# A gated state-space block and a routed expert block in one kernel: one routing pass behind the scan, D times u and the residual in PSUM, 19 weight splits inside the scan

## What is computed

```python
x = x + tanh(g_xattn) * ssm(ctx_1024, layernorm(x))
x = x + tanh(g_ffn) * moe(layernorm(x))
# ssm, per batch row: u = silu(conv(in_proj(ctx)) + conv_b); dt_lo, B, C = x_proj(u)
#   delta = softplus(dt_proj(dt_lo) + dt_proj_b)
#   state = state * exp(delta * A) + (delta * u) * B      # scan over 256 positions, 16 states
#   y = (sum over states of state * C + D * u) * silu(z)  # z = layernorm(x), transposed back at the end
# moe: logits = x @ gate_w; softmax over the best 2 of 8; sum of cw_e * (silu(x @ w0_e) * (x @ w1_e)) @ wo_e
```

## Time and profile before

| | us |
|---|---|
| median of 3 runs (340.27 to 341.49) | 341.0 |
| the profiled execution | 341.57 |
| its span, first to last instruction | 339.8 |
| set-up, to the first product of the scan | 0 to 38.3 |
| scan, to the end of the last scan instruction | 38.3 to 181.6 |
| behind the scan, to the first expert product | 181.6 to 212.5 |
| expert stage | 212.5 to 339.8 |

### The profile page before, as it was taken

How to read it: one execution, slowest core, us unless ns; L and a number is a source line. 1 busy time by engine, 2 the same in 40 slices (tenths; PEclk the granted TensorE clock), 3 DMA queues, 4 the chain that set the end, 5 groups by cost and what they waited for, 6 DMA issues and landing times.

```text
span 339.8 us, 4549 instructions
## 1 busy us (share of the span) xinstructions
PE 265.8 (78%) x1093; PEld 174.1 (51%) x1094; DVE 246.7 (73%) x450; ACT 176.8 (52%) x327; POOL 185.0 (54%) x162
## 2 busy tenths in 40 slices
PE   3976687747898857574866957999999999999960
PEld 4522142313444414232321645798899889988950
DVE  3757999999999896989995886356655655565540
ACT  2495386545476549344667061245655565566540
POOL 4001348995799759293999403234465446545331
PEclk9987558997999789696999775799999999999996
DMA  6799000000000000300007731112332333233221
GB/s 192 241 379 379 7 1 0 2 1 0 0 1 0 2 1 0 123 1 0 0 2 237 254 126 32 39 22 50 64 48 48 60 62 46 46 62 62 30 23 25
DMA packets 18910, 22.69 MB, mean 67 GB/s; under 512 B 2624, under 2 KB 14062, under 8 KB 18894
## 3 DMA queue, kind: packets, MB, share of 16 engines
q1 hardware_dynamic: 13312, 16.39, 13.9%
q0 software_dynamic: 4416, 6.03, 11.0%
q10 hardware_dynamic: 1166, 0.08, 0.2%
HBM read 17.38 MB, written 5.11 MB: 66 GB/s over the span
## 4 chain that ended last, share of the span: by engine, by line
PE 48%; DVE 20%; issue 13%; POOL 8%; ACT 5%; DMA 2%; POOLq 1%; SPq 0%; DVEq 0%; ACTq 0%
PE PD L865 10%; PE PZ L901 10%; PE PU L865 10%; PE PY L733 7%; POOL hC L390 7%; DVE states L1036 5%; DVE states L1042 4%; PE PY L887 3%; DMA xs<-in_x 2%; PE PY L695 2%; PE PZ L858 2%; PE PU L725 2%; POOL W_lo L381 1%; PE PY L847 1%; PE PU L842 1%
## 5 line engine op out<-in xcount | busy, mean ns | idle before, releaser
L390 POOL TENSOR_TENSOR hC<-states,WO 128x512 f32<-128x512 f32 x64 | 82.6, 1304 | 35.7 <-PE PY L733 20.4
L733 PE MATMUL PY<-hC,ident 128*128 128x512 f32 x128 | 78.9, 702 | 12.8 <-POOL hC L390 12.4
L1042 DVE TENSOR_TENSOR_SCAN states<-PD,states 128x512 f32<-128x512 f32 x64 | 77.5, 1212 | 0.2 <-ACT PD L541 0.2
L425 POOL DMA_INDIRECT out<-lg,y_at x23 | 36.4, 1585 | 55.8 <-ACT lg L627 52.2
L541 ACT ACTIVATE PD<-WO,Aneg 128x510 f32<-128x510 f32 x64 | 44.0, 688 | 40.0 <-DVE states L1042 35.8
L1309 DVE TENSOR_TENSOR WO_lo<-WO,WO_hi 128x512 fp32r<-128x512 f32 x46 | 29.8, 689 | 34.5 <-ACT WO_hi L620 33.9
L620 ACT ACTIVATE WO_hi<-WO 128x512 fp32r x46 | 26.5, 624 | 47.0 <-PE PZ L901 46.8
L1036 DVE TENSOR_TENSOR states<-PU,WO 128x512 f32<-128x512 f32 x64 | 43.0, 673 | 2.5 <-POOL hC L390 2.4
L725 PE MATMUL PU<-BC,sel 128*128 128x512 f32 x32 | 20.5, 640 | 28.7 <-DVE states L1036 28.7
L733 PEld LDWEIGHTS PY<-hC,ident 128*128 128x128 f32 x128 | 26.3, 224 | 29.8 <-POOL hC L390 24.5
L412 POOL DMA_INDIRECT hC<-x_rows,x_at x23 | 23.3, 1014 | 29.1 <-DVE x_at L1265 15.0
(11 more groups left out here) (221 smaller groups left out, 498.6 us busy)
## 6 DMA issues: line engine op xcount, KB each, us to landing
W<-in_L_ffn_w SPq DMA_DIRECT2D x16, 512.0 KB, 11.0
WO<-in_L_ffn_wo SPq DMA_DIRECT2D x8, 512.0 KB, 4.5
xs<-in_x SPq DMA_DIRECT2D x1, 1024.0 KB, 7.9
x_rows<-u SPq DMA_DIRECT2D x2, 512.0 KB, 2.8
out<-xs SPq DMA_DIRECT2D x2, 512.0 KB, 3.8
early<-in_ctx SPq DMA_DIRECT2D x1, 512.0 KB, 4.2
hC<-x_rows,x_at POOLq DMA_INDIRECT x23, 2.8
out<-lg,y_at POOLq DMA_INDIRECT x23, 3.8
```

The source lines that it names most:

```text
L390: pool.tensor_tensor(hC[:, n % 2, :], states[:, n % RING, :], C_rep[:, pair % C_RING, :], ALU.mult).then_inc(hc_done, 1)
L425: pool.indirect_dma_start(out=out, out_offset=bass.IndirectOffsetOnAxis(ap=y_at[:, s:s + 1], axis=0), in_=y_tile[s % 2], in_offset=None, c ...
L733: pe.matmul(PY[:, h, :], ident[:, :], hC[:, n % 2, :], start=(m == 0), stop=(m == DS - 1)).then_inc(y_done, 1)
L1042: dve.tensor_tensor_scan(states[:, n % RING, :], DEC[n % 2], states[:, n % RING, :], 0.0, ALU.mult, ALU.add).then_inc(scan_done, 1)
```

## The change

1. **Routing in one pass.** `places` and `ranks` run once, over 8 blocks of 128 rows and not twice over 4, behind the scan; `best_two` of the first half stands behind the last scan too. The two adds that make its logits (`logits_of`) stay inside, since TensorE wants the bank. `rows_hot` moves behind `places`, the slot table behind the table of rows.
2. **Skip in PSUM.** Each of the four sums in PY starts with a matmul of u by a diagonal matrix of D; the DVE instruction L1059 goes.
3. **Residual in PSUM.** TensorE puts x (`add_x`) and then the gated rows times tanh(g) (`add_gz`) into one bank; ACT copies the sum out (`x2_out`). DVE's L1070 goes, and the two halves of `turn_gz` become real matmuls.
4. **Softplus of the second half.** The relu and the 1 + e of `rounding` go from DVE to ACT, which writes the latter into PSUM.
5. **Splits.** 19 inside the scan, after steps 4, 7, ... 58 (before 24, from step 34 on after every second one), 4 on POOL behind it, 2 and 7 on DVE (before 4 and 4).
6. WARM from (2, 3, 1) to (1, 3, 1); the tables of steps are new.

```diff
+TURN_X_AT, X_OUT_AT, BASE_AT, BASE_OUT_AT = (17, 29), (22, 34), (23, 35), (28, 40)
+ADD_X_AT, ADD_GZ_AT, X2_OUT_AT = ((41, 42), (56, 57)), (43, 44), 49
+ROUTER_AT, LOGITS_AT, STATS_AT, RSTD_AT, ROOT_AT = 50, 53, (50, 51, 52), 55, 54
...
-WARM = (2, 3, 1)
+WARM = (1, 3, 1)
...
-SPLIT_AT = (4, 7, 10, 13, 16, 20, 24, 28, 32) + tuple(range(34, 64, 2))
-POOL_SPLITS = 28
+SPLIT_AT = tuple(range(4, 60, 3))
+POOL_SPLITS = len(SPLIT_AT) + 4
+DVE_SPLITS = (POOL_SPLITS, POOL_SPLITS + 2, len(SPLITS))
...
+            def x2_out(q):
+                for r in range(QB):
+                    b = q * QB + r
+                    act.wait_ge(x2_ps, b + 1)
+                    act.activation(xs[:, 2 * b:2 * b + 2, :].rearrange("p t d -> p (t d)"), PZ[r][:, :], ACT.Copy).then_inc(x2_ok, 1)
...
+            def plus_one(c):
+                act.wait_ge(relu_ok, c + 1)
+                act.wait_ge(sp_exp_ok, c + 1)
+                act.activation(DRAW[c], sp_exp[c], ACT.Identity, bias=1.0).then_inc(one_plus, 1)
...
+                if m == 0:
+                    if q:
+                        pe.wait_ge(gz_ok, h + 1)
+                    pe.wait_ge(diag_ok, 2)
+                    pe.matmul(PY[:, h, :], diag_D[:, h, :], u[:, q, h, :], start=True, stop=False)
                 pe.wait_ge(hc_done, n + 1)
-                if q and m == 0:
-                    pe.wait_ge(gz_ok, h + 1)
-                pe.matmul(PY[:, h, :], ident[:, :], hC[:, n % 2, :], start=(m == 0), stop=(m == DS - 1)).then_inc(y_done, 1)
+                pe.matmul(PY[:, h, :], ident[:, :], hC[:, n % 2, :], start=False, stop=(m == DS - 1)).then_inc(y_done, 1)
...
+            def add_x(q, r):
...
+                for l in range(2):
+                    pe.matmul(PZ[r][:, l * DX:(l + 1) * DX], ident[:, :], xs[:, q * QBLK + 2 * r + l, :], start=(l == 0), stop=False)
+
+            def add_gz(q, r):
+
+                pe.wait_ge(gz_ok, 2 * q + 2)
+                for l in range(2):
+                    for h in range(2):
+                        at = l * DX + h * P
+                        mm = pe.matmul(PZ[r][:, at:at + P], zs[:, q * QBLK + 2 * r + h, l * P:(l + 1) * P], scaled_id[:, :], start=False, stop=(l == 1 and h == 1))
+                mm.then_inc(x2_ps, 1)
...
+            for h in range(2):
+                dve.tensor_scalar(diag_D[:, h, :], ident[:, :], cols[:, 2, h:h + 1], None, ALU.mult).then_inc(diag_ok, 1)
+            dve.tensor_scalar(scaled_id[:, :], ident[:, :], tg[:, 0:1], None, ALU.mult).then_inc(gc_ok, 1)
...
-            through(RSTD_AT, BEST_AT)
-            best_two(0)
-            through(BEST_AT, PLACE_AT)
-            places(0)
-            through(PLACE_AT, NT)
-            gated(1, 0, 2)
-            gated(1, 1, 3)
+            through(RSTD_AT, NT)
+            best_two(0)
+            gated(1, 0)
+            gated(1, 1)
+            logits_of(1)
             best_two(1)
-            residual(1, 0)
-            residual(1, 1)
+            chosen_two()
+            link(dve.tensor_tensor(gap[:, :], top[:, :, 1], top[:, :, 0], ALU.subtract))
+            lower(DVE_SPLITS[0], DVE_SPLITS[1])
+            row_stats(1, 0)
+            row_stats(1, 1)
             variance(1)
+            places()
             rows_hot(dve, 0)
-            places(1)
             rows_hot(dve, 1)
```

More of the change, by code:

```diff
@@ L582, in _ @@
             act.wait_ge(c_ps, NT // 2)
-            for i in range(len(SPLIT_AT), len(SPLITS)):
+            for i in range(len(SPLIT_AT), DVE_SPLITS[1]):
                 upper(i)
+            x2_out(1)
             root(1)
@@ L588, in _ @@
             act.activation(egap[:, :], gap[:, :], ACT.Exp).then_inc(egap_ok, 1)
+            for i in range(DVE_SPLITS[1], DVE_SPLITS[2]):
+                upper(i)
             act.wait_ge(table_set, 1)
@@ L813, in _ @@
             base_logits(1)
-            through(BASE_AT[1] + 1, TURN_GZ_AT + 1)
-            turn_gz(0)
-            through(TURN_GZ_AT + 1, ROUTER_AT + 1)
-            router(0)
-            through(ROUTER_AT + 1, RANKS_AT + 1)
-            ranks(0)
-            through(RANKS_AT + 1, NT)
+            at = BASE_AT[1] + 1
+            for r in range(QB):
+                through(at, ADD_X_AT[0][r] + 1)
+                add_x(0, r)
+                at = ADD_X_AT[0][r] + 1
+            for r in range(QB):
+                through(at, ADD_GZ_AT[r] + 1)
+                add_gz(0, r)
+                at = ADD_GZ_AT[r] + 1
+            through(at, ROUTER_AT + 1)
+            router(0)
+            at = ROUTER_AT + 1
+            for r in range(QB):
+                through(at, ADD_X_AT[1][r] + 1)
+                add_x(1, r)
+                at = ADD_X_AT[1][r] + 1
+            through(at, NT)
             def keep_warm(n):
@@ L829, in _ @@
             router(1)
-            turn_gz(1)
+            for r in range(QB):
+                add_gz(1, r)
             pe.wait_ge(dbu_done, NT)
@@ L833, in _ @@
             keep_warm(WARM[0])
-            ranks(1)
+            ranks()
             keep_warm(WARM[1])
@@ L1126, in best_two, with lower @@
                 link(ins)
-                dve.tensor_tensor(mask[:, q, :, :], hot[:, q, 0, :, :], hot[:, q, 1, :, :], ALU.add).then_inc(mask_ok, 1)
+                dve.tensor_tensor(mask[:, :, :, :], hot[:, :, 0, :, :], hot[:, :, 1, :, :], ALU.add).then_inc(mask_ok, 1)
+            def lower(at, end):
+                for i in range(at, end):
+                    dve.wait_ge(W_hi_ok, i + 1)
+                    dve.tensor_tensor(lo_part(i), whole_part(i), hi_part(i), ALU.subtract).then_inc(W_lo_dve, 1)
             def mark(ins):
@@ L1181, in places @@
+                need(tiled)
+                ends = mark(dve.tensor_tensor_scan(tile_end[:, :], ones[:, 0:E], tiles[:, :], 0.0, ALU.mult, ALU.add))
                 need(chosen)
[L1182 to L1186 removed]
@@ L1210, in _ @@
-            drive(0)
-            through(0, 2)
-            relu(2)
-            through(2, 3)
-            relu(3)
-            through(3, 8)
+                summed = mark(dve.tensor_reduce(of_n(rank_f), picked[:, :, :, :, :].rearrange("p q k t e -> p (q k t) e"), AX_X, ALU.add))
+                need(ends)
+                starts = mark(dve.tensor_tensor(first_slot[:, :], tile_end[:, :], tiles[:, :], ALU.subtract))
+                dve.wait_ge(rstd2_ok, 2 * NQ)
+                dve.tensor_tensor(gap[:, :], gap[:, :], rstd[:, 1, :], ALU.mult).then_inc(gap_ok, 1)
```

268 lines of the change are left out of this document (119 added, 149 removed).

## The result

The changed kernel takes **323.02 us** (median of 4 runs, 320.57 to 324.10) against 341.23 (340.27 to 341.49) for the kernel before, measured beside it: a ratio of 0.9475, 95% interval 0.9424 to 0.9526. Forecast were 321.7 and a range of 315 to 329. The profiled execution took 322.93, its span is 321.2. Medians are over all runs of a kernel; ratios and intervals leave out the runs that lie more than 1.5% above its fastest, which are three of the six of r49_warm9 and one each of router49 and old_splits.

What follows compares the result with a forecast made beforehand. DVE, at 1.713 us a step, bounds the scan, with POOL pacing from step 34. Scan 20.1 - 4.2 = 15.9 off and 4.0 off behind it, from 341.57, gave 321.7 us; range 315 to 329.

Steps and rivals of the forecast that it cites:

- Work taken off DVE in the scan, 20.1: In the scan: relu, rounding, skip, residual, best two, places and waits for POOL leave DVE, together 20.1 us off.
- `add_x`, `add_gz`, router, 1.2, bounds 0 and 3: In the scan: 0.85 us pieces on a PE with 15% idle at full clock cost 1.2 us, bounds 0 and 3.
- The diagonal at the start, 2.3, bounds 0 and 4.5: At the scan's start: two diagonal matmuls at half clock delay the second sum, so DVE stands 2.3 us, bounds 0 and 4.5.
- Steps 32 and 33, 0.7: In the scan at steps 32 and 33: a diagonal behind the gate makes a new wait of 0.7 us.
- Splits, 1.4: In the scan: a split each third step stops POOL pacing, barely; 1.4 of DVE's 2.4 us of waits for POOL go.
- Behind the scan, last hC 3.65 off: Last scan's end to last gate product: with no split before the last hC, 2.65 us instead of 6.30, 3.65 off.
- the list of signs: Trace signs: scan end near 166, DVE idle 3 to 6 us before L1036, last hC within 0.3, expert product 27 later.
- From the gate to the first expert product, 0.35 off: Last gate product to first expert product: 24.63 us before, 0.35 off, bounds 3 either way; DVE's seven splits end before PE needs them.
- the first: Rival: TensorE falls behind at the two starts of the sums, diagonals at 4.5 and 2, others 1.5 more: 327; chance 0.18.
- The fourth: Rival: POOL's waits for PE's sums eat its margin, POOL paces the scan at 1.84 from step 17: 328; chance 0.06.
- The fifth: Rival: PE's clock stays at half and bounds the scan: 357; queue 84 at full clock, break-even 80%; chance 0.02.
- The third: Rival: the stretch behind the scan does not shrink, 325.7; four DVE instructions blocked behind POOL splits, 3.7; chance 0.09.

Runs made afterwards that it cites:

- r49_warm9: The changed kernel with the first half's router at step 49, not 50, and nine idle TensorE matmuls, not three, before the tables: 318.66 us.
- router49: The changed kernel with the first half's router one step earlier in PE's queue, at step 49 and not 50: 321.01 us.
- old_splits: The changed kernel with the old table of splits, 24 inside the scan and 28 on POOL in all: 326.71 us.
- b_routing_behind: The kernel before with best two and places of the first half moved behind the last scan, still in two passes: 340.96 us.
- warm9: The changed kernel with nine instead of three idle TensorE matmuls between the mask sums and the tables: 321.93 us.
- pool28: The kernel of r49_warm9 with nine instead of four trailing splits on POOL and four instead of nine on DVE: 322.88 us.
- skip_dve: The changed kernel with D times u back on DVE and without the diagonal on TensorE: 323.97 us.
- behind_pause: The kernel of b_routing_behind with POOL's four trailing splits held back until the first half's row numbers stand: 335.53 us.

## Why the prediction was right, step by step

The forecast missed by 1.3 us. The profiled execution sets the stages against the sum: the scan is 15.0 shorter (predicted 15.9), the stretch behind it 3.8 (predicted 4.0). The main mechanism was right: work and waits leave DVE, which paces the scan. That the number came so close is in part luck, since single terms were off by up to 4 and cancelled: in the scan 1.4 more came off than counted and the diagonals cost 1.9 less, while the `add` pieces and the router cost 4.2 more.

Which of the six changes brings how much is shown for some only: the splits 3 to 5, the skip in PSUM about 1 if anything, the first half's routing moved by itself nothing. The residual, the softplus and the joined routing pass have no run of their own.

- **Work taken off DVE in the scan, 20.1.** The waits left in the scan sum to 6.5 (the five rows above), and 15.0 + 6.5 = 21.5 came off. What is over is POOL: I counted 1.4 of its 2.4 us of waits, and all of them went, as did the 0.2 for ACT; those in the rows above are new.
- **`add_x`, `add_gz`, router, 1.2, bounds 0 and 3.** This is the term that failed. The `add` pieces cost at most the 0.77 at 134.10 and the 0.49 at 158.94; the router cost 4.12, outside my bounds. The step said that such pieces cost what they last on a PE with 15% idle. router49 shows that the price was that of a queue: PE behind ACT's copy, ACT behind two table loads. The 3.41 idle that stood there before was the hint. The sum counted it as gone, inside the 5.1 for the best two, although the two adds that wait for the router stay in the scan. In b_routing_behind these adds go behind the scan as well, and the wait is gone there.
- **The diagonal at the start, 2.3, bounds 0 and 4.5.** In the changed kernel's execution the waits are 1.1. Those of warm9, router49, r49_warm9, pool28 and old_splits, the same code up to there, are 2.2 to 2.7, so the size was right and the changed kernel's execution a lucky one. The whole part is worth 1 us in skip_dve, by medians whose intervals overlap. **Steps 32 and 33, 0.7:** no wait stands there.
- **Splits, 1.4.** Undersized when taken alone: 4.9 in the kernel before. In the changed one they are worth 3.0 to 3.7, of which 2.0 come with the last hC, which the sum had as a term of its own.
- **Behind the scan, last hC 3.65 off.** From the last scan's end to the last gate product are 3.39, not 2.65: 2.9 off. POOL starts the last hC 0.9 late, where the list of signs had at most 0.3, and the cast before the gates waits for it, 1.23 us. That the first half's best two "hides in this wait" held, with 0.47 us to spare (the wait ahead of the second gate product).
- **From the gate to the first expert product, 0.35 off.** 0.87 off. One step of it was wrong: DVE's seven splits should end before PE needs them. They take 4.29 us and end at 193.28, 0.9 behind PE's second table, and the split of x and the first product follow. This fits warm9, where the 5.57 us for which PE stands before the tables were filled without a measurable gain.

Of the rivals, the first has the right shape, TensorE late, and the wrong place: not the starts of the sums, but the router at step 50. The fourth is out: POOL's longest stretch without a gap is 12.8 us, before it was 30.7. The fifth is out too (granted clock 0.90 in the scan, 0.86 before). Its 84 us for the queue at full clock do not follow from the earlier trace rows, where PE is busy for 22.84 us in some 16 steps, which makes about 93 for 64; that moves its break-even from 80% to 78% and changes nothing else. The third had put 3.7 us on the port for four DVE instructions that meet POOL's last splits. In the changed kernel this did not come: POOL's run ends at 174.11, just before the masks (0.36 for two and 0.23), and only the two casts lose 1.06 and 0.40. In b_routing_behind the port cost 7.6 and in pool28 4.55. Of the list of what would show it, the last scan's end (167.0, forecast 166), POOL's gaps and the 27 us held. The last hC did not start within 0.3 us, and the waits ahead of L1036's successor were 1.7, not 3 to 6: they lie at steps 6, 9 and 60, none at 36 to 40, and the stall stood ahead of the logits.

## What to carry to other kernels

Price a piece that is put into an in-order queue by what stands ahead of it and what that waits for, two engines deep, and not by its length: here one step's difference was worth 4 us of DVE's waits and 2 to 3.3 us of the kernel's time. Before work is moved behind a loop, look at what the neighbour on the shared port does there, and count the moved work that nothing covers: two passes moved as they were gained nothing. And test parts by themselves and not by their share in a sum that fits: the splits were worth two to three and a half times their term, and the routing alone, for which I had expected 8 us, nothing. Before a difference between two profiled executions is put down to an edit, look whether it shows in kernels without the edit too.

## What the runs showed of the hardware

- A DVE instruction can be held up by POOL well past one of POOL's instructions. In two kernels, b_routing_behind and behind_pause, a cast of 128x8 lasted 7.78 and 2.90 us, past six and two ends of POOL's instructions, and finished with the last of the run. In five others (the first cast, 1.23 us in the changed kernel, 0.80 in r49_warm9 and 0.89 in old_splits, and 0.53 in b_splits_routing and 0.57 in pool28) it got in at the first such end, though POOL's run went on. That the run is the cause in the first case is what behind_pause shows: with a shorter run the cast is shorter by 4.9. The Trainium skill, page SBUF — State Buffer, section Who interferes with whom, names casts among the operations that can take the ports shared with GpSimd and says that the later to issue blocks fully. The traces agree for the casts that waited for the one POOL instruction already running, and the two-input instructions hot, mask and gap waited for one each too. The two long casts do not fit it: POOL's next instructions started 0.36 us and more behind the cast and went ahead of it. Which of two waiting engines gets the ports when an instruction ends, the runs leave open: the two long casts were issued 0.36 us ahead of POOL's next start, all others 0.47 or more.
- The same program's scan stage differs by some 2 us between executions (128.3 in the changed kernel, 130.6 in warm9), and the moment at which TensorE's clock rises differs with it. The first product starts at 38.7 in both the changed kernel and pool28, with the same code there, and these are their windows, in this order:

```profile
46.70:47.70 1.00, 1.00 (x4) 0.62 (x3) 1.00 (x2) 0.99 (x2) 0.18 (x1) 0.95 0.03 8
46.70:48.70 2.00, 2.00 (x4) 1.00 (x3) 1.30 (x2) 1.84 (x3) 0.76 (x1) 0.50 0.01 4
```

  The clock is at its upper level (1.00, and 0.50 is the lower) 8 us behind the first product in the changed kernel, and only after 10 to 11 in pool28, router49, warm9, r49_warm9 and old_splits. DVE's first waits are 1.2 us in the former and 2.2 to 2.7 in the latter five. What makes the clock rise earlier in one execution is not shown.
- The expert stage starts with the lower level in every kernel. The clock rises 3 to 6 us behind the first product: 3.0 in warm9, but also in behind_pause, 4.5 in r49_warm9, 6.0 in the changed kernel and router49.
